# Routed expert rows in blocks of 128: 16 slots of two blocks and 7 of one block, with GpSimd out of that stage

## The reference

```python
gate_logits = jnp.einsum('bsd,ed->bse', x, gate_w) + gate_b + expert_bias
top_idx = jnp.argmax(gate_logits, axis=-1)
for e in range(NUM_EXPERTS):                    # 8 experts, D_FF = 1024
    mask = (top_idx == e)[..., None].astype(x.dtype)
    h = jax.nn.relu(jnp.einsum('bsd,df->bsf', x, w1[e]) + b1[e])
    y = jnp.einsum('bsf,fd->bsd', h, w2[e]) + b2[e]
    out = out + mask * y
```

## Time and profile before

| | us |
|---|---|
| median of 3 runs | 1138.78 |
| lowest and highest run | 1137.65, 1141.77 |
| span of the profiled execution | 1137.6 |
| TensorE busy | 1076.8 (95%) |
| VectorE busy | 823.7 (72%) |
| ScalarE busy | 597.2 (53%) |
| GpSimd busy | 517.2 (45%) |

### The profile page before, as it was taken

One profiled execution on the slowest core, in us unless ns is written; L12 is line 12 of the kernel. 1 busy time (PEld: TensorE's weight loads), 2 busy tenths in 40 slices (PEclk: granted clock), 3 DMA queues, 4 the chain that ended last, 5 costly groups with the idle time before them and its releaser, 6 DMA issues. The chain is left out here.

```text
span 1137.6 us, 21065 instructions
## 1 busy us (share of the span) xinstructions
PE 1076.8 (95%) x6874; PEld 962.4 (85%) x6874; DVE 823.7 (72%) x1289; ACT 597.2 (53%) x1060; POOL 517.2 (45%) x376
## 2 busy tenths in 40 slices
PE   6999999999999999999989779999999999999995
PEld 5998988889898988887677579999999998888884
DVE  5865656575665656576895678888888886788777
ACT  4554444444444444454555545566656664666663
POOL 3444444435344444434638743344334434744445
PEclk9999999999999999999999889999999999999997
DMA  5235010111102012031354647667766764323213
GB/s 171 63 108 198 1 55 37 37 55 37 55 10 82 0 55 74 9 121 55 148 226 168 224 154 226 208 207 231 223 211 205 233 216 139 122 93 110 101 47 111
DMA packets 86401, 137.35 MB, mean 121 GB/s; under 512 B 9313, under 2 KB 68193, under 8 KB 85345
## 3 DMA queue, kind: packets, MB, share of 16 engines
q1 hardware_dynamic: 76112, 122.48, 32.3%
q0 software_dynamic: 3072, 8.39, 2.2%
q10 hardware_dynamic: 7184, 6.08, 1.6%
HBM read 99.64 MB, written 37.29 MB: 120 GB/s over the span
## 5 line engine op out<-in xcount | busy, mean ns | idle before, releaser
L635 POOL TENSOR_TENSOR acc<-acc,ytmp 128x512 f32<-128x512 f32 x120 | 156.7, 1306 | 251.8 <-ACT ytmp L723 238.0
L1486 POOL TENSOR_TENSOR w_l<-raw,w_h 128x1024 fp32r<-128x1024 f32 x46 | 113.6, 2492 | 171.5 <-ACT w_h L1346 171.5
L1319 ACT ACTIVATE act_o<-ps,scan_bias 128x512 f32<-128x512 f32 x192 | 129.3, 687 | 111.1 <-PE ps L357 88.5
L787 DVE SCALAR_TENSOR_TENSOR hT_l<-ps,hT_h 128x512 fp32r<-128x512 f32 x128 | 87.8, 686 | 116.5 <-ACT hT_h L686 116.5
L723 ACT ACTIVATE ytmp<-ps,sel 128x256 f32<-128x256 f32 x256 | 107.4, 471 | 102.3 <-PE ps L934 101.7
L355 PE MATMUL ps<-x1T,WB_h 128*128 (+1 forms) x384 | 153.4, 400 | 4.0 <-POOL WB_l L506 2.8
L357 PE MATMUL ps<-x1T,WB_l 128*128 (+1 forms) x384 | 152.0, 396 | 0.0
L356 PE MATMUL ps<-x1T,WB_h 128*128 (+1 forms) x384 | 151.1, 394 | 0.0
L932 PE MATMUL ps<-vals_h,hT_h 128*128 128x256 f32 x512 | 145.5, 284 | 2.4 <-DVE hT_l L787 2.3
L934 PE MATMUL ps<-vals_h,hT_l 128*128 128x256 f32 x512 | 144.1, 282 | 0.0
L933 PE MATMUL ps<-vals_l,hT_h 128*128 128x256 f32 x512 | 144.1, 281 | 0.0
(11 more groups left out here) (197 smaller groups left out, 2774.2 us busy)
## 6 DMA issues: line engine op xcount, KB each, us to landing
raw<-w SPq DMA_DIRECT2D x46, 1024.0 KB, 5.4
x1T<-xT_d SPq DMA_DIRECT2D x16, 512.0 KB, 4.3
comb_b<-comb_d SPq DMA_DIRECT2D x8, 1024.0 KB, 7.2
xs_d<-zeros ACTq DMA_DIRECT2D x1, 5888.0 KB, 21.0
rows<-xs_d SPq DMA_DIRECT2D x23, 256.0 KB, 4.7
y_d<-y_sb SPq DMA_DIRECT2D x23, 256.0 KB, 5.2
x_in<-x SPq DMA_DIRECT2D x8, 512.0 KB, 3.9
x_d<-x SPq DMA_DIRECT2D x8, 512.0 KB, 4.2
```

Of the source, the lines that this page charges most:

```text
L635: pool.tensor_tensor(dst[:, 2:4, :], acc[:, 2:4, :], ytmp[:, k % 2, :, :], ALU.add).then_inc(acc23, 1)
L1319: act.activation(act_o[:, i % 2, w, :], ps[:, 3 * (i % 2) + w, :], func, bias=scan_bias[:, w, i:i + 1]).then_inc(act_g, 1)
L1486: pool.tensor_tensor(w2_l[:, j, :], raw2[:, j, :], w2_h[:, j, :].bitcast(F32), ALU.subtract).then_inc(w2_lo, 1)
```

## The change

Rows are now laid out in blocks of 128 instead of 256. An expert with n rows gets its pairs of blocks (n rounded up to 128, then by twos) and, where their number is odd, one single block. The 16 slots of two blocks hold the pairs; the singles follow, first in slots of two blocks that no pair needs, then in the 7 slots of one block. The order is a round of big, big, small, seven times, then two big ones; the hardware loop runs over rounds 1 to 6. Slot by slot each engine now does the following.

- TensorE: as before, with 128 moving rows and one row block in the small slots (first layer 48 products of 128 columns, second layer 24 of 256). It signals the second layer in two halves (`l2_part`).
- ScalarE: also makes `eT_h` (`round_e`). Its copies of w1 and w2 are spread over the slot, half by half.
- VectorE: no longer makes `eT_h`; takes over the low part of w2 from GpSimd. y of a slot is now taken out at the start of the next.
- GpSimd: nothing in this stage.
- SyncE: each weight matrix in two DMAs of 512 KB, each with a semaphore of its own, waiting for its half alone; w1 and w2 are laid out on the host so that a half is one contiguous piece for each partition.
- VectorE's routing arithmetic grows: blocks, pairs and singles of each expert, the places of the singles, and the slot table.

The core of the diff:

```diff
-NSLOT = T // SLOT + E1 - 1
+N_BIG, N_SMALL = T // SLOT, E1 - 1
+NSLOT = N_BIG + N_SMALL
+N_BLOCK = T // P + E1 - 1
+ROUND = 3
+N_ROUND = (NSLOT + 1) // ROUND
...
+    def blocks(r, k):
+
+        r, k = r + k // ROUND, k % ROUND
+        return (4 * r + ST * k, ST) if k < ST else (T // P + r, 1)
+
+    def every_slot(slot, eng):
+
+        for k in range(ROUND):
+            slot(0, k)
+        with eng.Fori(1, N_ROUND - 1) as r:
+            for k in range(ROUND):
+                slot(r, k)
+        for k in range(NSLOT - ROUND * (N_ROUND - 1)):
+            slot(N_ROUND - 1, k)
+
+    def left(r, k):
+
+        return NSLOT - 1 - ROUND * r - k if isinstance(r, int) else NSLOT
...
+            def raw2_half(n, h, e):
+                if not zero(n):
+                    wait_alone(sp, w2_lo, 2 * (n - 1) + h + 1)
+                j = slice(h * HALF2, (h + 1) * HALF2)
+                sp.dma_start(raw2[:, j, :],
+                             a["w2"][bass.ds(e, 1), h].rearrange("a p j d -> p (a j) d")).then_inc(r2_in[h], 16)
...
+            def load_b1(n, e):
+                if not zero(n):
+                    wait_alone(sp, t_ok, FJ * n)
                 sp.dma_start(b1c[:], a["b1"][bass.ds(e, 1)].rearrange("a p j -> p (a j)")).then_inc(b1_in, 16)
...
+            def store_y(r, k):
+
+                wait_alone(sp, ys_ok, ROUND * r + k + 1)
+                b, st = blocks(r, k)
+                sp.dma_start(y_v[bass.ds(b, st)].rearrange("b p d -> p b d"), y_sb[:, 0:st, :]).then_inc(y_st, 16)
+
...
+            def slot(r, k):
+
+                n = ROUND * r + k
+                if not zero(n):
+                    store_y(*((r, k - 1) if k else (r - 1, ROUND - 1)))
+                load_b2(n)
+                if left(r, k) > 0:
+                    e = expert(n + 1)
+                    raw2_half(n + 1, 1, e)
+                    if left(r, k) > 1:
+                        load_rows(r, k + 2)
+                    load_b1(n + 1, e)
+                if left(r, k) > 1:
+                    e = expert(n + 2)
+                    raw1_half(n + 2, 0, e)
+                    raw1_half(n + 2, 1, e)
+                    raw2_half(n + 2, 0, e)
 
...
+            def slot(r, k):
+
+                n, (_, st) = ROUND * r + k, blocks(r, k)
+                W = st * P
+                pe.wait_ge(sT_ok, n + 1)
...
                         for c in range(DC):
-                            last_mm = mm3(pe, ps[:, q, (j % 2) * SLOT:(j % 2 + 1) * SLOT], w1_h[:, c, f], w1_l[:, c, f],
-                                          sT_h[:, c, :], sT_l[:, c, :], c == 0, c == DC - 1)
+                            last_mm = mm3(pe, ps[:, q, (j % 2) * W:(j % 2 + 1) * W], w1_h[:, c, f], w1_l[:, c, f],
+                                          sT_h[:, c, 0:W], sT_l[:, c, 0:W], c == 0, c == DC - 1)
                     last_mm.then_inc(l1_full, 1)
...
+                    for i in range(st):
+                        t = slice(i * P, (i + 1) * P)
                         dst = ps[:, 4 + i, 0:D]
-                        pe.matmul(dst, eT_h[:, j, r], w2_h[:, j, :], start=j == 0, stop=False)
-                        pe.matmul(dst, eT_h[:, j, r], w2_l[:, j, :], start=False, stop=False)
-                        last_mm = pe.matmul(dst, eT_l[:, j, r], w2_h[:, j, :], start=False, stop=j == FJ - 1)
-                last_mm.then_inc(l2_full, 1)
+                        pe.matmul(dst, eT_h[:, j, t], w2_h[:, j, :], start=j == 0, stop=False)
+                        pe.matmul(dst, eT_h[:, j, t], w2_l[:, j, :], start=False, stop=False)
+                        last_mm = pe.matmul(dst, eT_l[:, j, t], w2_h[:, j, :], start=False, stop=j == FJ - 1)
+                    if j in (HALF2 - 1, FJ - 1):
+                        last_mm.then_inc(l2_part, 1)
...
             for g in range(B_FIRST):
                 body(g)
             pe.wait_ge(act_g, 3 * MC * B_FIRST - 3)
-            slot(0)
-            with pe.Fori(1, NSLOT - 1) as s:
-                slot(s)
-            slot(NSLOT - 1, True)
+            every_slot(slot, pe)
...
+            def round_e(n, q, W):
+                act.wait_ge(t_ok, FJ * n + 2 * (q + 1))
+                j = slice(2 * q, 2 * q + 2)
+                act.activation(eT_h[:, j, 0:W], t32[:, j, 0:W], ACT.Copy).then_inc(e_hi, 1)
+
+            def slot(r, k):
+                n, (_, st) = ROUND * r + k, blocks(r, k)
+                w2_half(n, 1)
+                for q in range(FJ // 2):
+                    relu(n, q, st * P)
+                    round_e(n, q, st * P)
+                    if q == 1 and left(r, k) > 0:
+                        w1_half(n + 1, 0)
+                if left(r, k) > 0:
+                    rows_hi(r, k + 1)
+                    w1_half(n + 1, 1)
+                    w2_half(n + 1, 0)
 
             g = GROUPS - 1
...
-            def w2_half(s, h):
-                pool.wait_ge(w2_hi, 2 * s + h + 1)
-                j = slice(h * HALF2, (h + 1) * HALF2)
-                pool.tensor_tensor(w2_l[:, j, :], raw2[:, j, :], w2_h[:, j, :].bitcast(F32), ALU.subtract).then_inc(w2_lo, 1)
-
-            with pool.Fori(0, NSLOT) as s:
-                for h in (0, 1):
-                    w2_half(s, h)
-
             pool.wait_ge(y_st, 16 * NSLOT)
...
+                for half in (0, 1):
+                    link(dve.tensor_tensor(cnt16[:, half], incl[:, :, TILES - 1:TILES].to_broadcast(r),
+                                           k256[:, half, :].unsqueeze(1).to_broadcast(r), ALU.is_gt))
+                link(dve.tensor_reduce(nblk[:], cnt16[:], AX.X, ALU.add))
+                pairs = nblk[:, 1, :]
+                link(dve.tensor_tensor_scan(pend[:], ones[:, 0:E1], pairs, 0.0, ALU.mult, ALU.add))
+                link(dve.tensor_tensor(single[:], nblk[:, 0, :], pairs, ALU.subtract))
+                link(dve.tensor_tensor_scan(send[:], ones[:, 0:E1], single[:], 0.0, ALU.mult, ALU.add))
+                link(dve.tensor_scalar(out=past[:], in0=pend[:, E1 - 1:E1], scalar1=float(N_BIG), scalar2=None, op0=ALU.max))
+                link(dve.scalar_tensor_tensor(out=yblk[:], in0=send[:], scalar=pend[:, E1 - 1:E1], in1=single[:],
+                                              op0=ALU.add, op1=ALU.subtract))
+                link(dve.tensor_scalar(out=ymin[:], in0=yblk[:], scalar1=-float(N_BIG), scalar2=0.0, op0=ALU.add,
+                                       op1=ALU.min))
+                link(dve.scalar_tensor_tensor(out=sblk[:], in0=yblk[:], scalar=past[:, 0:1], in1=ymin[:],
+                                              op0=ALU.add, op1=ALU.add))
+                link(dve.tensor_tensor(pair0[:], pend[:], pairs, ALU.subtract))
+                link(dve.tensor_scalar(out=pair0[:], in0=pair0[:], scalar1=float(SLOT), scalar2=None, op0=ALU.mult))
+                link(dve.tensor_scalar(out=pair1[:], in0=pend[:], scalar1=float(SLOT), scalar2=None, op0=ALU.mult))
+                link(dve.scalar_tensor_tensor(out=shift[:], in0=sblk[:], scalar=float(P), in1=pair1[:],
+                                              op0=ALU.mult, op1=ALU.subtract))
...
+                link(dve.tensor_tensor(incl[:], incl[:], pair0[:].unsqueeze(2).to_broadcast((P, E1, TILES)), ALU.add))
                 link(dve.tensor_tensor(rt1[:], cum, incl[:].rearrange("p e t -> p t e"), ALU.add))
+                t = (P, TILES, E1)
+                link(dve.tensor_tensor(over[:], rt1[:], pair1[:].unsqueeze(1).to_broadcast(t), ALU.is_ge))
+                link(dve.tensor_tensor(over[:], over[:], shift[:].unsqueeze(1).to_broadcast(t), ALU.mult))
+                link(dve.tensor_tensor(rt1[:], rt1[:], over[:], ALU.add))
                 link(dve.tensor_tensor(rt1[:], rt1[:], onehot[:], ALU.mult))
                 link(dve.tensor_reduce(rmax[:], rt1[:], AX.X, ALU.add))
                 dve.tensor_copy(pos_i[:], rmax[:]).then_inc(r_pos, 1)
...
+                se = (P, N_ROUND * ROUND, E1)
+                first_row = x_io[:].rearrange("p r k -> p (r k)").unsqueeze(2).to_broadcast(se)
+                link(dve.tensor_scalar(out=sblk[:], in0=sblk[:], scalar1=float(P), scalar2=1.0, op0=ALU.mult, op1=ALU.add))
+                link(dve.tensor_tensor(sblk[:], sblk[:], single[:], ALU.mult))
+                link(dve.tensor_scalar(out=sblk[:], in0=sblk[:], scalar1=-1.0, scalar2=None, op0=ALU.add))
+                link(dve.tensor_tensor(in0[:], pair0[:].unsqueeze(1).to_broadcast(se), first_row, ALU.is_le))
+                link(dve.tensor_tensor(in1[:], pair1[:].unsqueeze(1).to_broadcast(se), first_row, ALU.is_le))
+                link(dve.tensor_tensor(in0[:], in0[:], in1[:], ALU.subtract))
+                link(dve.tensor_tensor(in1[:], sblk[:].unsqueeze(1).to_broadcast(se), first_row, ALU.is_equal))
+                link(dve.tensor_tensor(in0[:], in0[:], in1[:], ALU.add))
+                link(dve.tensor_tensor(in0[:], in0[:], e_io[:].unsqueeze(1).to_broadcast(se), ALU.mult))
+                link(dve.tensor_reduce(sef[:], in0[:], AX.X, ALU.add))
```

(40 more changed lines are left out.)

254 lines of the change are left out of this document (109 added, 145 removed).

## The result

The changed kernel takes 1093.41 us (median of 4 runs, 1092.73 to 1094.46) against 1139.07 of the kernel before (4 runs, 1137.65 to 1141.77): a ratio of 0.960, 95% interval 0.959 to 0.962. Faster by 45.7 us, where 39 were forecast. The profiled execution has a span of 1091.1 us, 46.5 less than that of before.

The account below looks back on a forecast made before the run. TensorE, busy 1076.8 of 1137.6 us, was taken to bound the kernel. Terms -11.6 (big slots), -27.8 (small slots), -3.0 (slot 0) and +3.5 (routing) sum to -38.9: span 1098.7, forecast 1100 us, range 1092 to 1138.

Parts of the forecast that it names:

- The case forecast: Whole kernel: waits in big slots go, narrow products take 0.112 us; 1100 us (1092 to 1106), chance 0.62.
- slot 0: First slot of the stage: second layer no longer waits 2.18 us for eT_l; gain 3.0 us, bounds 0 and 4.5.
- up to slot 0: Routing arithmetic before pos_i: longer, wholly on the path to the first slot; cost 3.5 us, bounds 2 and 6.1.
- Big slots: 15 two-block slots: the 0.85 us wait before the second layer goes, 12.67 to 11.9 us each; gain 11.6 us.
- Small slots: 7 one-block slots: first layer 5.4 us, second 2.85, slot 8.7 instead of 12.67; gain 27.8 us.
- rival B: Small slots' first layer: narrow product costs the fp32 price, 10.7 us, slot 14.0; 1137 us, no change; chance 0.17.
- ScalarE's margin: ScalarE in big slots: about 10.4 us of work, under TensorE's 11.9 by only 1.5 us.
- rival F: Narrow product goes by its columns, 0.065 us, first layer 3.1; 2.3 us less in each round, 1084 us; chance 0.04.
- Transfers: Weight DMAs: 8.0 MB per round in 32.5 us, 246 GB/s, halves asked for early enough; cost 0.
- Rival C: Transfers bound the round: at 219 GB/s it takes 36.5 us; 1130 us, in part 1110 to 1130; 0.10 with E.
- D: Narrow load and product don't overlap, at the fp32 price: 0.33 us, small slot 19.1; 1173 us, slower; chance 0.07.
- E: Routing or ScalarE trailing TensorE eats the gain: big slots 12.4, small ones 9.5; 1113 us; counted with Rival C, together 0.10.

Follow-up runs that it names:

- 192-column run: The changed kernel with 192 instead of 128 columns moving in the small slots' first layer (64 leftovers, results not read): 1093.52 us, ratio 0.960.
- fp32 experiments: Changed kernel, small slots' first layer as 16 plain fp32 products instead of 48 fp32r: 1090.41 us; with VectorE also copying w2's second half there: 1090.15 us.
- the run with 3.7 more: The changed kernel with eight more VectorE instructions of 256 elements ahead of pos_i, results not used: 1097.28 us, ratio 0.963.
- The run on the kernel before: The kernel before with only w2's low part moved from GpSimd to VectorE, 23 wide slots and whole loads kept: 1114.89 us, ratio 0.978.
- fp32 run: The changed kernel with the small slots' first layer as 16 plain fp32 products, VectorE copying w1 and the rows whole there: 1090.41 us, ratio 0.957.

## Why the prediction was right

It said 1100 us and faster; it came to 1093.41, 6.6 less and 1.4 above the lower end of its range. The case forecast is the one that happened: no gap at the seams, narrow products at 0.11 us. Its terms against the two profiled executions, in the order of the sum:

| term | forecast us | measured us | from |
|---|---|---|---|
| 15 big slots and 7 small ones | -39.4 | -44.9 | 278.8 to 233.9 |
| slot 0 | -3.0 | -2.9 | 17.3 (657.69 to 675.0) to 14.4 (658.85 to 673.3) |
| up to slot 0 | +3.5 | +1.2 | its first product, 657.69 to 658.85 |
| behind the stage | 0 | +0.1 | 183.8 to 183.9 |
| sum | -38.9 | -46.5 | spans |

**Big slots, the largest error.** 11.9 was forecast, 11.59 is the mean: 4.7 of the 7.6 us. The reason for the gain (the wait goes) was right, the terms of what stays were too large: 0.44 for four transposes and 0.08 for seams. From start to start the transposes take 0.35, ahead of a small slot there are two only, 0.14, and there is no seam. So 11.72 and 11.50. A transpose does cost the 0.11 forecast; but the first product behind them stands 0.20 ahead of its next one instead of 0.12, and this piece was already in the 5.70 of the second layer, so the sum had it twice. "It can't be under 11.8" was wrong for this reason and for the other: a bound made of rows must use the size of the step as changed, here the transposes of a one-block slot. The statement that quarter 1 and 2 are late next, by 1.5 us, doesn't follow from its own times either: ready 3.6, 5.1, 7.5, 8.9 against 6.1, 7.5, 9.0, 10.4 leaves 1.5 to the third and the fourth, which are the tight ones in the trace too.

**Small slots.** 8.7 forecast, 8.58 measured: first layer 48 x 0.1106 = 5.31 for 5.4, second layer 2.89 for 2.85, transposes 0.38 for 0.44. The choice of 0.112 over the 0.222 of rival B was the one that decided the case. Its reason, that the load sets the price, is borne out in part: the 192-column run shows that the moving columns don't, the load itself wasn't varied. The clock stayed at its upper level (1.00, so 2.4 GHz) though the array streams half as long: that worry was idle.

**ScalarE's margin.** That ScalarE stays under TensorE, in big slots by only 1.5 us, held: it is 203 of 234 us busy, and TensorE never waits for it. The fp32 experiments show that edge. With a first layer of 3.57 us the small slot would have been 6.8; ScalarE's chain took 1.24 of the 1.74 us back, the kind of bound that rival F's sum had.

**Transfers.** Cost 0 was right in the result. The prediction did reckon the distance for w1's first half in a small slot, 5.0 us from request to use; it is 6.1. Rival C had the wrong form: it asked for bandwidth, and the round runs at 241 GB/s, above its 219. What can bind here is the time from the request to the use of a buffer's new content, 3.5 us in a narrow slot with one whole buffer against 5 for a load. The prediction booked the halves as "their own waits" and gave them no price; undone, they cost 21 us. This step was the weakest, and that it came out right is partly luck: the halves are what lets the narrow slots pay. With halves these bring 24.1 us (1117.52 to 1093.41), with whole loads 4.3 (1119.0 to 1114.69).

**Routing.** The arithmetic grew as forecast: from the first instruction of `slot_rows` to `pos_i` 6.28 us before (582.54 to 588.82) and 9.85 after (580.90 to 590.75), +3.57 against 3.5. That it is all on the path is shown by the run with 3.7 more. Slot 0 came only 1.2 us later, for two reasons. This execution reached the routing 1.64 us earlier, 1.0 of it already by 65 us from the start, in a stage that the change doesn't touch. That is scatter of single executions: the first scatter stands anywhere from 589.79 to 593.58 us in the eleven profiled kernels that have the changed routing and nothing more ahead of it. The other is the way from the first scatter to slot 0, 67.60 to 67.67 us in all twelve with the changed routing and 68.34 and 68.38 in the two with the old one: 0.7 us less, the cause of which is open. So the routing costs 3.57 - 0.7, some 2.8 us, and 1.6 of the 2.3 us of this line is luck.

**Slot 0.** 2.9 for 3.0, but the parts differ. The wait of 2.4 us went, as forecast; the second layer took 5.84 us at a granted clock of 1.00 instead of 7.26 at 0.76; the first layer took 8.26 instead of 7.28, with a granted clock of 0.66 over it. The sum was the same with all slots wide (14.46 us), where the first layer took 7.58 and 0.57 of wait was left.

**What took the wait away.** I put it to GpSimd's instructions on VectorE's path. The run on the kernel before bears that out there: -24 us with this one move. But in the changed kernel GpSimd could come back for 2 us. So the gain has no single owner.

**Rivals.** B and D (the narrow product at the fp32 price or beyond) fell with 0.1106 us. C and E fell with a stage without gaps. F fell with 0.1106 where it had 0.065, and with the 192-column run.

## What to carry to other kernels

An fp32r product with a fresh load of 128 x 128 weights costs 0.11 us here, whether 128 or 192 columns move: halving the moving side saved 7% of the first layer (5.69 to 5.31 us), while the second, whose number of products fell, was halved. Where the moving side is that short, count products with their loads and not columns, and see whether fewer, dearer products (plain fp32) win. Before a stage is made shorter, list for each single buffer the time from the request of its load, at its release or later, to the next use and hold it against the landing time of its load: that distance shrinks with the stage, and splitting the load in halves with semaphores of their own gives it back. Where a contended instruction stretches, ask how much slack its result has before booking the stretch as time. Before an instruction is taken off an engine's list, ask whether the one behind it can start earlier at all.

## What the runs showed of the hardware that was not expected

- An fp32r product of 128 and of 192 moving columns goes at 0.1106 and 0.111 us (5.31 and 5.33 us for 48), one of 256 at 0.118. The three records are 274, 275 and 281 ns long.
- A plain fp32 product of 128 columns is two records of 0.1116 us, so 0.223, against 0.332 for the three fp32r products that replace it: at this width plain fp32 is the cheaper form for TensorE.
- A load of 128 columns isn't always the 0.107 us that the prediction drew from the earlier trace rows: over 12 partitions, with 12 columns moving, such loads follow each other at 0.06 us.
- VectorE in the fp32 run: a plain copy of 128x1024 between two SBUF tensors takes 0.69 us, a subtraction of the same size 1.23.

```profile
712.02 0.69 DVE L1704 COPY w_f<-raw 128x1024 f32<-128x1024 f32 x1
...
716.84 1.23 DVE L1724 TENSOR_TENSOR w_l<-raw,w_h 128x1024 fp32r<-128x1024 f32 x1 [0.95 <-ACT w_h L1415]
```

- 512 KB land in 5.1 us in this stage, hardly sooner than 1 MB (5.4 in the earlier trace rows, 4.9 with w1 alone whole): halves don't land earlier, they can be asked for earlier.
